# One operation for the high part of W_e's first slice, its identity in PSUM, and later loads that wait for the first tiles of x

## The reference

```python
u = jax.nn.gelu(cond @ W_proj + b_proj, approximate=False)
logits = (u @ W_u)[:, None, :] + jnp.einsum('bnd,dc->bnc', x, W_e)
return x + logits
```

## Time and profile before

| | |
|---|---|
| median of 3 runs | 344.46 us (344.3 to 344.85) |
| the profiled execution's own time | 344.53 us |
| its span, first to last instruction | 342.4 us |
| TensorE matmul busy | 338.1 us, 99% of the span |
| VectorE busy | 263.6 us, 77% |
| ScalarE busy | 249.1 us, 73% |
| GpSimd busy | 283.7 us, 83% |
| mean DMA rate over the span | 206 GB/s |

### The profile page before, as it was taken

The page is one execution under the profiler, slowest core; times in us unless marked ns, Lnnn a source line. Parts: engine busy times, 40 slices in busy tenths (PEclk is TensorE's granted clock), DMA queues, the critical chain, the costliest instruction groups (busy, mean ns, idle before and its releaser), DMA issues.

```text
span 342.4 us, 7876 instructions
## 1 busy us (share of the span) xinstructions
PE 338.1 (99%) x2703; PEld 329.7 (96%) x2703; DVE 263.6 (77%) x302; ACT 249.1 (73%) x428; POOL 283.7 (83%) x203
## 2 busy tenths in 40 slices
PE   8999999999999999999999999999999999999996
PEld 4869999999999999999999999999999999999996
DVE  2989997777887777887777789777788877778811
ACT  3677787778777777877777877777787777787741
POOL 2499999988889898889898888989888888888860
PEclk9999999999999999999999999999999999999999
DMA  7998799878888977888997787898878799787216
GB/s 260 314 196 211 167 235 242 232 200 215 200 184 199 241 219 198 209 204 169 230 230 219 195 214 184 184 245 217 217 186 222 175 208 245 202 208 205 92 48 231
DMA packets 73353, 70.64 MB, mean 206 GB/s; under 512 B 2944, under 2 KB 68480, under 8 KB 69248
## 3 DMA queue, kind: packets, MB, share of 16 engines
q1 hardware_dynamic: 73344, 70.53, 81.5%
HBM read 36.96 MB, written 33.55 MB: 206 GB/s over the span
## 4 chain that ended last, share of the span: by engine, by line
PE 98%; DMA 1%; ACT 0%; issue 0%
PE banks L857 31%; PE banks L861 30%; PE banks L859 30%; PE banks L783 2%; PE banks L825 2%; PE banks L843 1%; DMA head_raw<-in_x 1%; PE banks L768 1%; PE banks L764 1%; PE banks L821 0%; PE banks L818 0%; PE banks L815 0%; ACT y L597 0%
## 5 line engine op out<-in xcount | busy, mean ns | idle before, releaser
L857 PE MATMUL banks<-t_hi,hi 128*128 128x256 f32 x496 | 140.6, 283 | 0.1
L861 PE MATMUL banks<-t_hi,lo 128*128 128x256 f32 x496 | 140.4, 283 | 0.0
L859 PE MATMUL banks<-t_lo,hi 128*128 128x256 f32 x496 | 140.4, 283 | 0.0
L857 PE MATMUL banks<-w_hi,hi 128*128 128x256 f32 x372 | 105.4, 283 | 0.0
L859 PE MATMUL banks<-w_lo,hi 128*128 128x256 f32 x372 | 105.3, 283 | 0.0
L861 PE MATMUL banks<-w_hi,lo 128*128 128x256 f32 x372 | 105.3, 283 | 0.0
L602 DVE STREAM_TRANSPOSE work<-quad_raw 128x1024 f32<-128x1024 f32 (+1 forms) x62 | 100.6, 1623 | 0.0
L857 PEld LDWEIGHTS banks<-t_hi,hi 128*128 128x128 f32 x496 | 95.2, 192 | 0.3 <-issue 0.2
L859 PEld LDWEIGHTS banks<-t_lo,hi 128*128 128x128 f32 x496 | 95.2, 192 | 0.0
L861 PEld LDWEIGHTS banks<-t_hi,lo 128*128 128x128 f32 x496 | 95.2, 192 | 0.0
L353 POOL TENSOR_TENSOR lo<-work,hi 128x1024 fp32r<-128x1024 f32 x31 | 75.0, 2418 | 16.9 <-ACT hi L454 16.9
(11 more groups left out here) (81 smaller groups left out, 411.4 us busy)
## 6 DMA issues: line engine op xcount, KB each, us to landing
out<-y SPq DMA_DIRECT2D x31, 1024.0 KB, 4.5
quad_raw<-in_x SPq DMA_DIRECT2D x120, 256.0 KB, 5.7
w_e<-in_L_cond_weight_matrix SPq DMA_DIRECT2D x2, 512.0 KB, 5.9
w_proj_sb<-in_L_cond_W_proj SPq DMA_DIRECT2D x2, 512.0 KB, 7.9
w_u<-in_L_cond_weight_matrix SPq DMA_DIRECT2D x1, 1024.0 KB, 8.5
quad_raw<-in_x SPq DMA_DIRECT2D x8, 128.0 KB, 8.1
out<-y SPq DMA_DIRECT2D x3, 256.0 KB, 2.2
head_raw<-in_x SPq DMA_DIRECT2D x1, 512.0 KB, 3.7
```

The source lines that it names most:

```text
L857: pe.matmul(psum[:, t, :], a_hi[:, 2 * j + t, :], b_hi[:, j, :], start=False, stop=False, skip_group_check=True)
L859: pe.matmul(psum[:, t, :], a_hi[:, 2 * j + t, :], b_lo[:, j, :], start=False, stop=False, skip_group_check=True)
L861: last = pe.matmul(psum[:, t, :], a_lo[:, 2 * j + t, :], b_hi[:, j, :], start=False, stop=(j == T - 1), skip_group_check=True)
```

## The change

Slice 0 of W_e: GpSimd makes a second identity, 128 x 512, with ones at the columns 4p of partition p, in the SBUF of `bias` (which is not in use then), and ScalarE copies it into PSUM (the bank of `h_psum`). VectorE adds slice 0 and this identity and writes w_hi of slice 0 in one operation. The diagonal of slice 0 in W_e itself, which the low part and the sums of W_e need, is added by GpSimd after that. Zeros matmuls after the transposes: 3 instead of 8. SyncE waits for tiles 0 and 1 to land before it issues cond and everything behind it. TensorE's 24 head matmuls stand in another order, with tile 0's low part of slice 0 second. In the first quad the rounding of S3 on ScalarE stands behind the copy that seeds the B bank, and the sum S3 on VectorE behind the first evacuation of the head.

```diff
-WARM_ON = 8
+WARM_ON = 3
...
+        first_eye = bias[:, :]
+        eye_psum = h_psum
...
             for n in range(2):
                 load_w_e(n)
+
+            sp.wait_ge(direct_loaded, 16)
             sp.dma_start(cond_sb[:, :], cond).then_inc(cond_loaded, 16)
...
+            pool.memset(first_eye, 0.0).then_inc(first_eye_zeroed, 1)
+            pool.wait_ge(first_eye_zeroed, 1)
+            pool.affine_select(out=first_eye, in_=first_eye, compare_op=ALU.not_equal, fill=1.0,
+                               base=0, pattern=[[-1, C]], channel_multiplier=NJ).then_inc(first_eye_ready, 1)
             pool.wait_ge(ident_ready, 1)
-            for j in range(1, NJ):
-                pool.wait_ge(w_e_loaded[j // 2], 16)
+            def add_ident(j, done):
                 diag = diagonal(j)
-                pool.tensor_tensor(diag, diag, ident[:, :], ALU.add).then_inc(w_diag_ready, 1)
+                pool.tensor_tensor(diag, diag, ident[:, :], ALU.add).then_inc(done, 1)
+            pool.wait_ge(w_e_loaded[0], 16)
+            add_ident(1, w_diag_ready)
+            pool.wait_ge(w_hi_ready[0], 1)
+            add_ident(0, first_diag_ready)
+            pool.wait_ge(w_e_loaded[1], 16)
+            for j in range(2, NJ):
+                add_ident(j, w_diag_ready)
...
+            act.wait_ge(first_eye_ready, 1)
+            act.copy(eye_psum, first_eye).then_inc(first_eye_copied, 1)
             for n in range(T):
                 direct_hi(n)
...
                 act.copy(b_bank, a_bank[p]).then_inc(b_seeded, 1)
                 if early:
+                    hi_s3(k, p, True)
                     snap_c(k, p, first)
...
             hi_s2(0, 0, True)
-            hi_s3(0, 0, True)
...
-            dve.wait_ge(ident_ready, 1)
+            dve.wait_ge(first_eye_copied, 1)
             dve.wait_ge(w_e_loaded[0], 16)
-            first_diag = diagonal(0)
-            dve.tensor_tensor(first_diag, first_diag, ident[:, :], ALU.add).then_inc(first_diag_ready, 1)
-            dve.wait_ge(first_diag_ready, 1)
-            dve.tensor_copy(w_hi[:, 0, :], w_e[:, 0, :]).then_inc(w_hi_ready[0], 1)
+            dve.tensor_tensor(w_hi[:, 0, :], w_e[:, 0, :], eye_psum, ALU.add).then_inc(w_hi_ready[0], 1)
             split_direct(0)
             split_direct(1)
+            dve.wait_ge(first_diag_ready, 1)
...
             sum_s1(0, 0, True)
-            sum_s3(0, 0, True)
...
             evacuate(0, slice(0, 1))
+            sum_s3(0, 0, True)
             evacuate(0, slice(1, T))
...
+            def low(j, t):
+                if j == 0:
+                    pe.wait_ge(direct_lo_ready, t + 1)
+                product(t, x_lo[0], w_hi, j)
+
+            def low_w(j, last=False):
+                pe.wait_ge(w_lo_ready[j], 1)
+                for t in range(T):
+                    end = product(t, x_hi[0], w_lo, j, last=last)
+                return end
 
             high(0)
-            for j in range(NJ + 1):
...
+            low(0, 0)
+            high(1)
+            low(0, 1)
+            for j in range(1, NJ):
+                for t in range(T):
+                    low(j, t)
+                if j == NJ - 1:
+                    pe.wait_ge(cond_loaded, 16)
+                    flip(flip_psum, by_j(cond_sb[:, :]), cond_flipped)
+                low_w(j - 1)
                 if j + 1 < NJ:
                     high(j + 1)
...
+            low_w(NJ - 1, last=True).then_inc(multiplied, 1)
```

More of the change, by code:

```diff
@@ L177, in build_cond_residual @@
         w_diag_ready = sem("w_diag_ready")
+        first_eye_zeroed = sem("first_eye_zeroed")
+        first_eye_ready = sem("first_eye_ready")
+        first_eye_copied = sem("first_eye_copied")
         first_diag_ready = sem("first_diag_ready")
@@ L790, in high @@
                     product(t, x_hi[0], w_hi, j, first=(j == 0))
-            high(0)
-            for j in range(NJ + 1):
+            def low(j, t):
[7 more added lines that the diff above has]
+                return end
+            high(0)
+            low(0, 0)
[8 more added lines that the diff above has]
+                low_w(j - 1)
                 if j + 1 < NJ:
                     high(j + 1)
[L797 to L809, removed]
+            low_w(NJ - 1, last=True).then_inc(multiplied, 1)
             pe.wait_ge(cond_hi_ready, 1)
```

## The result

The changed kernel takes 346.44 us (median of 22 runs, 344.73 to 348.73) against 344.58 (22 runs, 343.98 to 347.45). The ratio is 1.0047, 95% interval 1.0032 to 1.0063: slower by about 1.6 us by the ratio, 1.9 by the medians. I had forecast 344.4 and a range to 345.1. Its times are also more scattered than those of before: half of them lie between 345.6 and 347.2.

What follows compares the result with a forecast made beforehand. TensorE bounds (98%), its steady part's start also set by VectorE's chain from the landing at 21.4. TensorE gains 0.47, then 0.27; VectorE's chain 0, so at best 0.05: forecast 344.4, own range 344.1 to 344.7, wider 343.8 to 345.1.

Steps and rivals of the forecast that it cites:

- Loads behind the wait: Step on SyncE's DMA issues: cond and all behind go out 2.4 us later; expected effect on landings 0.
- So the line absorbs the 2.4 us: First quad's loads stand in line up to 8.1 us, so issuing 2.4 us later should not delay their landing at 21.4.
- The bound that I set beside it: Worst case for the DMA landings: +2.3 us if they move with their issue; 0 if the line stays filled.
- I take 0 for both: Neither a loss from later issue (up to +2.3) nor a gain from an undisturbed stream (0.7 at best) was counted.
- Two of the signs that I had named: Forecast wrong if VectorE's second-half transposes start before 21.2 or after 21.8, TensorE doesn't wait at m5, or W_e lands before 6.4.
- Rival B: The DMA queue runs dry and the first quad's second half lands late: 345.5 at half the bound, 346.8 whole; chance 0.12.
- The hole of 0.3 us: Possible gap in the DMA stream before cond's data, if some 2 us of fixed cost lay ahead: 344.8.
- Rival A: W_e and the first quad's second half land 0.3 to 0.7 sooner: 344.0, at best 343.7; chance 0.24.
- a second chain: Beside TensorE's: DMA landing at about 21.4, 21 us of VectorE, then TensorE's m5 and m7 of quad 1.
- The stall of 0.2 for tile 0's low part: TensorE, in the head matmuls after slice 0's high part, would wait 0.2 us for VectorE's low part at 8.07.
- The wait at 35.13 goes: TensorE's long piece of 0.26 us at 35.13 would vanish, as S2 and GpSimd's low parts come 0.6 earlier.
- S3 behind the evacuation: Moving VectorE's sum S3 back by 3 us would bring S2 and the low part of S1 0.6 us earlier.

Runs made afterwards that it cites:

- e5: Changed kernel with cond and W_proj issued at once, SyncE waiting for W_e's first half before the second tiles and all behind: 345.03 us.
- e1: Kernel before with only SyncE's wait for tiles 0 and 1 added ahead of cond and all behind: 1.5 us slower.
- e4: Changed kernel with SyncE waiting for W_e's first half instead of tiles 0 and 1: 349.11 us.
- e2: Changed kernel without SyncE's wait: 344.85 us, ratio 1.0002 to the kernel before.
- e7: Changed kernel without the wait, second tiles and first quad loaded as whole rows in 4 KB packets (values not right): 344.79 us.
- e8: Changed kernel without the wait and without the two low passes of head tile 3 on TensorE (result incomplete): 344.92 us.
- e6: Changed kernel with its wait, second tiles and first quad loaded as whole rows in 4 KB packets (values not right): 345.77 us.
- e11: Changed kernel with its wait, plus one tiny early load from W_proj's rows on ScalarE's queue: 346.56 us.
- e9: Changed kernel without the wait, without head tile 3's low passes, three of four head evacuations cut to 16 columns (result incomplete): 344.05 us.
- e3: Changed kernel with SyncE's wait moved behind the issues of cond and W_proj, ahead of the second tiles: 344.86 us.
- e10: Changed kernel without the wait, ScalarE copying the bias out of PSUM, sum S3 back ahead of S2: 344.62 us, ratio 1.0001 to before.

## Why the prediction was wrong

**The step that failed** is "Loads behind the wait", and in it "So the line absorbs the 2.4 us" and "I take 0 for both". The bound that I set beside it, +2.3 if landings move with their issue, is the size of what came: the landing of the first quad's second half moved by 2.42 in the profiled execution, and the median time by 1.86. It came in another way, though. The issues themselves caught up: those of the first quad began at 9.84, 1.2 later and not at 11, and ended at 18.04, 5.9 us before the last landed. I had argued from the length of the line, and the line was long enough. What I left out is that a line of 16 engines has 16 ends, and that the stream itself can slow down while it is full. A load is there when its slowest part is, and the rows that I had show only that last part and the mean rate. Two of the signs that I had named came: that VectorE's transposes start after 21.8, and W_e before 6.4 (its first half at 6.33). The second means little, for it landed at 6.30 in e5, without a wait ahead of cond, and at 6.43 in e1.

**Rival B** had the right sign, the right place and the right price (it named m7 and VectorE's chain, one for one, 345.5 to 346.8) but the wrong mechanism: the queue did not run dry. It had 0.12. The hole of 0.3 us that I had worked out from a fixed cost does not show in the changed kernel, where cond, issued at 4.19, landed at 8.3, 0.3 us sooner than before; a hole shows only in e4, with a wait 2.3 us longer. Rival A's premise, that issuing slows the stream, fell: in e4 nothing is issued between 2.1 and 6.5, and in its rates of the first 24 us, in 40 slices of 0.6 us, the eighth to tenth (from 4.2 us) still fall to 198, 253 and 355:

```profile
GB/s 0 0 20 123 369 362 348 198 253 355 382 205 61 229 406 307 225 328 389 311 282 175 215 263 167 351 234 382 373 265 132 120 176 226 215 224 224 225 229 218
```

**Right**: the reading that a second chain, from a landing through VectorE, sets TensorE's entry into the steady part, when the landing is late. With an earlier landing (e2, e7) the chain is as long, but it is held at the copy of the bias, by W_u's matmuls; I had not seen that. In eleven of the thirteen traces, of kernels with medians from 344.6 to 349.1, the span is 306.6 or 306.7 more than the start of one VectorE operation, and e8 shows that TensorE's saved time is waited out. Also right: the operation of 0.68 took 0.69; product started at 7.17 in the changed kernel (forecast 7.47, with W_e landed 0.3 sooner); three zeros matmuls left a gap and the clock did not fall (PEclk 1.00 from 6 to 14 us): TensorE was idle for 0.70 us at 6.5, and the matmuls behind it start 0.23 us apart (8.12, 8.35, 8.59 in the changed kernel), as in the earlier trace rows.

**Smaller misses.** The stall of 0.2 for tile 0's low part did not come: in e2 its matmul starts at 7.85, 0.26 behind the one before it. The matmuls of h start at 13.65 in e2, 0.30 before the 13.95 of before and not 0.47. W_u's matmuls came 0.12 earlier, not 0.27: ScalarE's Gelu gained less. "The wait at 35.13 goes" is wrong: it is 0.20 at 35.02 in e2. GpSimd was ahead, but then waited 0.47 us for ScalarE's rounding of quad 1's upper half:

```profile
32.36 2.42 POOL L374 TENSOR_TENSOR lo<-work,hi 128x1024 fp32r<-128x1024 f32 x1 [0.47 <-ACT hi L477]
```

S3 behind the evacuation was to bring 0.6 us; the low part of the first quad's S1 starts 0.70 earlier in e2, of which 0.52 is the earlier landing. The select that I took at 1.2 us took 0.61, for four times the columns of the 0.29 in the earlier trace rows.

**Open.** Why a later issue makes the parts fall apart. Shown: it does so with at least 15 packets in flight (the changed kernel), without small packets (e6, though with a smaller spread: 1.9 us for W_proj's second half, 1.3 in e7), not by the first access to the memory (e11), more by the lateness of cond and W_proj than by that of the loads behind (e5), and in e9 without a wait. In the trace's packet records of the changed kernel, the 4 KB packets that start between 8 and 9 us, W_proj's, take 307 ns on average where before they took 186; what they wait for no view shows. That is not the cause in general: in e1 and e11, which lose as much, they take 174 and 167. How the parts land in the executions that were not profiled is not known, and cond and W_proj were not held back one without the other.

## What to carry to other kernels

Do not hold loads back to give earlier ones a clear path when they stand in line in order anyway: here W_e landed at the same time with or without the wait (its first half at 6.3 to 6.8 in all kernels), and 2.3 us of lead were lost for what was behind. When an engine has 98% of the chain, look for the last place where it waited a tenth of a microsecond: the chain behind that wait was as long here, and a delay there came out in full while a gain on the busy engine was swallowed. If a landing only just meets its reader, work out what it costs when it comes later as well as what it brings when it comes earlier, even if the queue looks full. And before moving an operation, look whether it covers a wait where it stands.

## What the runs showed of the hardware

The DMA share did not tell the queue's progress: from 8 to 14 us it was 0.97 to 1.25 with 268, 271 and 251 GB/s in the changed kernel, 1.01 to 1.15 with 385, 259 and 332 before. The distance between the first and the last part of W_proj's second half and of W_u was 0.8 to 1.3 us in before, e2, e3, e8 and e10, and up to 3.3 (W_u in e1; 3.0 in the changed kernel). The size of the packets did not set the pace of x's loads: from 14 to 22 us e7 moved 2.00 MB, with the first quad in 4 KB packets, and e2 1.99 MB, with it in 512-byte packets.

GpSimd's add on slice 1's diagonal took 0.52 beside VectorE's new operation, which has one input in PSUM, where it took 0.68 beside one with two inputs in SBUF:

```profile
6.47 0.52 POOL L345 TENSOR_TENSOR w_e<-w_e,ident 128x128 f32<-128x128 f32 x1 [3.77 <-DMA w_e<-in_L_cond_weight_matrix]
```

It is 0.52 or 0.53 in all eleven kernels with the new operation, and 0.69 in e1, which has the old one. This is what the Trainium skill (GPSIMD Engine Reference, Specifications) says of the shared SBUF interfaces; the trace agrees, with 0.16 us for this form.
